# The expert stage made sparse: tokens sorted by expert on the chip, scattered, multiplied in tiles of one expert, gathered back

## The reference

```python
logits = x @ gate_w.T
scores = jax.nn.sigmoid(logits) + gate_bias
group_scores = scores.reshape(T, G, E // G).max(axis=-1)       # 8 groups of 8 experts
_, sel_groups = lax.top_k(group_scores, TG)                    # the best 4 groups
masked_scores = scores * mask                                  # the other groups at 0
topk_w, topk_i = lax.top_k(masked_scores, K)                   # K = 6
topk_w = topk_w / (topk_w.sum(axis=-1, keepdims=True) + 1e-08)
comb = jnp.zeros((T, E), x.dtype).at[jnp.arange(T)[:, None], topk_i].add(topk_w)
h = jax.nn.silu(jnp.einsum('th,eih->eti', x, eg_w)) * jnp.einsum('th,eih->eti', x, eu_w)
routed = jnp.einsum('eti,ehi,te->th', h, ed_w, comb)
return (shared + routed).reshape(B, S, H)
```

## Time and profile before

| | |
|---|---|
| median of 3 runs | 2080.95 us (2079.45 to 2091.61) |
| profiled execution, first to last instruction | 2082.6 us |
| PE, DVE, ACT, POOL busy | 93%, 71%, 64%, 47% of the span |
| expert stage, from the last update of the cross attention | 1493 to 2082.6 us |

### The profile page before, as it was taken

The page is one execution under the profiler, slowest core; times in us unless marked ns, Lnnn a source line. Parts: engine busy times, 40 slices in busy tenths (PEclk is TensorE's granted clock), DMA queues, the critical chain, the costliest instruction groups (busy, mean ns, idle before and its releaser), DMA issues.

```text
span 2082.6 us, 46757 instructions
## 1 busy us (share of the span) xinstructions
PE 1926.8 (93%) x15317; PEld 1548.1 (74%) x15317; DVE 1486.0 (71%) x3968; ACT 1336.5 (64%) x3090; POOL 971.7 (47%) x1173
## 2 busy tenths in 40 slices
PE   6999999999999999985089999999899999999998
PEld 4877778888888888852087878787677777777776
DVE  4668767777666666658977787666787788677775
ACT  4676567777776777657746767777555555555554
POOL 2555544444444444310017656444366566566565
PEclk8999999999999999998599999899899999999999
DMA  6533300000000000000033444555233333333333
GB/s 178 170 111 112 105 2 2 2 2 2 2 2 2 2 2 2 2 1 1 0 92 108 125 123 120 150 149 152 73 119 119 122 119 123 119 121 122 122 125 95
DMA packets 139169, 161.12 MB, mean 77 GB/s; under 512 B 15340, under 2 KB 99244, under 8 KB 138796
## 3 DMA queue, kind: packets, MB, share of 16 engines
q1 hardware_dynamic: 132780, 153.46, 24.5%
q10 hardware_dynamic: 6160, 4.78, 0.7%
HBM read 119.75 MB, written 38.70 MB: 76 GB/s over the span
## 4 chain that ended last, share of the span: by engine, by line
PE 68%; issue 8%; POOL 8%; DVE 6%; ACT 4%; SPq 3%; DMA 2%; ACTq 0%; POOLq 0%; DVEq 0%
POOL h_lo L2273 7%; PE bank L1010 6%; PE bank L1026 6%; PE score_banks L279 6%; PE score_banks L999 5%; PE bank L951 5%; PE bank L952 4%; PE bank L953 4%; PE bank L290 3%; PE score_banks L1930 3%; PE score_banks L1928 3%; PE score_banks L1929 3%; PE score_banks L261 3%; PE bank L1928 2%; PE bank L1929 2%
## 5 line engine op out<-in xcount | busy, mean ns | idle before, releaser
L2273 POOL TENSOR_TENSOR h_lo<-h,h_hi 128x512 fp32r<-128x512 f32 x264 | 341.5, 1294 | 243.3 <-ACT h_hi L2054 243.1
L1449 POOL TENSOR_TENSOR pw<-ew,rw 128x410 f32<-128x410 f32 x256 | 222.9, 871 | 368.7 <-DVE rw L1299 368.7
L2047 ACT ACTIVATE sl<-score_banks 128x512 f32<-128x512 f32 x264 | 157.9, 598 | 237.2 <-PE score_banks L1930 235.8
L459 ACT ACTIVATE pt<-score_banks 128x512 f32<-128x512 f32 (+1 forms) x384 | 230.0, 601 | 114.8 <-PE score_banks L279 113.8
L2192 DVE TENSOR_TENSOR bank<-score_banks,sl 128x512 f32<-128x512 f32 x264 | 184.1, 697 | 143.3 <-PE score_banks L1930 115.0
L1163 ACT ACTIVATE ew<-score_banks,nmax 128x205 f32<-128x205 f32 x512 | 217.8, 435 | 103.1 <-DVE nmax L1292 101.9
L573 DVE TENSOR_REDUCE nmx<-score_banks 128x4 fp32r<-128x512 f32 (+1 forms) x288 | 171.4, 596 | 121.4 <-PE score_banks L261 118.5
L725 POOL TENSOR_SCALAR_AFFINE_SELECT pt<-pt 128x512 f32<-128x512 f32 x256 | 165.2, 646 | 163.2 <-ACT pt L459 163.2
L279 PE MATMUL score_banks<-q_pack,k_diag 128*128 128x128 f32 (+1 forms) x1536 | 238.6, 279 | 0.4
L279 PEld LDWEIGHTS score_banks<-q_pack,k_diag 128*128 128x128 f32 (+1 forms) x1536 | 189.9, 181 | 46.4 <-issue 38.0
L1928 PE MATMUL score_banks<-x_hi,w_hi 128*128 128x512 f32 x528 | 209.9, 398 | 0.0
(11 more groups left out here) (353 smaller groups left out, 4694.6 us busy)
## 6 DMA issues: line engine op xcount, KB each, us to landing
share_b<-share_rows SPq DMA_DIRECT2D x256, 256.0 KB, 3.1
q_rows<-q_hi SPq DMA_DIRECT2D x96, 128.0 KB, 2.7
q_pack<-q_rows SPq DMA_DIRECT2D x32, 384.0 KB
raw<-in_experts SPq DMA_DIRECT2D x33, 192.0 KB, 3.1
q_rows<-q_lo SPq DMA_DIRECT2D x48, 128.0 KB, 2.8
k_diag<-k_rows SPq DMA_DIRECT2D x64, 96.0 KB
q_pack<-q_rows SPq DMA_DIRECT2D x31, 192.0 KB
k_diag<-k_rows SPq DMA_DIRECT2D x124, 48.0 KB
```

What stands on the lines that cost most here:

```text
L459: nc.scalar.activation(m.pt[0:a.keys, c, :, :].rearrange("p h t -> p (h t)"), m.flip[c % 2][0:a.keys, :], ACT.Exp).then_inc(s.exped.semaph ...
L1449: nc.gpsimd.tensor_tensor(m.pw[:, n, :, :], m.ew[:, n % 2, :, :], m.rw[:, n % 2, :].unsqueeze(2).broadcast_to([128, 2, KW]), ALU.mult)\
L2273: nc.gpsimd.tensor_tensor(m.h_lo[:, k % 3, :], m.h[:, (k + u) % 2, :], m.h_hi[:, k % 3, :].bitcast(F32), ALU.subtract).then_inc(s.los, 1)
```

## The change

Only the chosen experts are computed. The steps are these.

- The order of a group's choices is worked out by PE and DVE: matmuls with a triangle of ones and a square of ones (`ranks`) count, for each token and expert, how many tokens of the chunk stand before it; DVE adds each expert's start, rounded up to 128 rows, and takes the six slots per token with its max instruction (`starts`, `slots`). A table says which expert each tile of 128 rows belongs to (`list_tiles`, `table`).
- POOL scatters each normalised row to its six slots in DRAM: one indirect DMA of 128 rows for each sequence and choice, 192 in all (`scatter`). It later gathers the results the same way, 192 more (`gather`), into a ring of four sequences (`GBUFS`).
- The eight groups form four chunks (`SPANS`) of 1, 3, 3 and 1 groups. Since the number of tiles depends on the data, each chunk has room for the worst case: 11, 17, 17 and 11 rounds of eight tiles, 56 rounds in all, each always run.
- A round reads 8 tiles (512 KB), transposes them on PE, loads eight expert offsets into registers, projects with those as addresses, takes silu (ACT) and product (DVE), transposes the hidden values (four transposes for eight tiles), projects down and writes 512 KB back. All in plain float32, one expert per matmul of 128 columns: eight up, eight down.
- DVE finds each choice's share (`shares`) and adds the six gathered rows by their shares (`combine`), sequence b in round 34 + b up to sequence 21, the last ten after the rounds, beside the shared part, which now stands at the end.
- The slots are cleared once, by four DMAs from a tile of zeros that SP issues after attention 0 (`clear_slots`, 56 x 512 KB in all). The weights are loaded whole in 26 pieces; POOL splits nothing.

The core of the diff (the sorting's arithmetic is left out):

```diff
 def moe_tensor(pe, nc, m, s):
+    def tiles_in(n):
+        pe.wait_ge(s.tile_in[n % XBUFS], 16 * (n // XBUFS) + 16)
+        for k in range(2):
+            for i in range(4):
+                last = nc.tensor.transpose(m.turn[k][:, 128 * i:128 * i + 128], m.xr[:, n % XBUFS, 4 * k + i, :], m.ident[:])
+            last.then_inc(s.tiles_t, 1)
+    def gate_up(n):
...
+        _, experts[n] = nc.values_load_multi_w_load_instructions(
+            m.erow[0:1, chunk, TILES * r:TILES * r + TILES], engines=(mybir.EngineType.PE,), min_val=0, max_val=(E - 1) * F,
...
+        wait(pe, s.products, n)
+        for j in range(TILES):
...
+            last = nc.tensor.matmul(m.both[:, j // 4, j % 4, :, :], m.xt8[:, 128 * j:128 * j + 128],
+                                    m.gate_up[:, :, bass.ds(experts[n][j], F)], start=True, stop=True)
+    def body(n):
+        chunk, r = ROUNDS[n]
+        if r == 0:
+            tiles_in(n)
+        gate_up(n)
+        between(n)
+        if n < LAST_OF[chunk]:
+            tiles_in(n + 1)
+        if r > 0:
+            down(n - 1)
+        turn_hidden(n)
+        after(n)
+        if n == LAST_OF[chunk]:
+            down(n)
...
+        for n in range(NR):
+            if n == FIRST_OF[1]:
+                table(2)
+                ranks(7)
+                table(3)
+            body(n)
+        shared_tokens(0)
...
+            shared_gate_up(g)
+            if g + 1 < G:
+                shared_tokens(g + 1)
+            if g > 0:
+                shared_down(g - 1)
 def moe_vector(dve, nc, m, s, cross, link):
+    def combine(b, added=0):
+        wait(dve, s.shared_added, added)
+        dve.wait_ge(s.fetched[b % GBUFS], 16 * EK * (b // GBUFS) + 16 * EK)
+        for k in range(EK):
+            wait(dve, s.combined, EK * b + k)
+            nc.vector.scalar_tensor_tensor(tok(m.x, b), m.yk[:, b % GBUFS, k, :], m.wk[:, EK * b + k:EK * b + k + 1], tok(m.x, b),
+                                           ALU.mult, ALU.add).then_inc(s.combined, 1)
+    def after(n):
+        if n == 0:
+            for i in range(NORM_STEPS):
+                norm_alone(nc, m, link, m.stats, m.rstd, m.shift, 128, LATE, i)
+        elif n == 1:
+            for g in range(4, 8):
+                normalise(g)
+        if n in (AHEAD + 2, AHEAD + 4, AHEAD + 6):
+            rank(3 + (n - AHEAD) // 2)
+        if AHEAD <= n < AHEAD + 8:
+            first = ROUTE_STEPS // 2 * ((n - AHEAD) % 2)
+            for i in range(first, first + ROUTE_STEPS // 2):
+                route(4 + (n - AHEAD) // 2, i)
+        if 0 <= n - FIRST_OF[1] < 16:
+            shares(n - FIRST_OF[1])
+        if 0 <= n - FIRST_OF[2] < 16:
+            shares(16 + n - FIRST_OF[2])
+        if 0 <= n - FIRST_OF[2] - 6:
+            combine(n - FIRST_OF[2] - 6)
     def run():
+        normalise(1)
+        rank(0)
+        starts(0)
+        list_tiles(0)
+        slots(0)
...
+        normalise(2)
+        normalise(3)
+        keep_table(0)
+        for n in range(ROUTE_STEPS):
+            route(1, n)
+        for g in (2, 3):
+            for n in range(ROUTE_STEPS):
+                if n == 4:
+                    rank(g - 1)
+                route(g, n)
+        rank(3)
+        starts(1)
+        list_tiles(1)
+        for g in (1, 2, 3):
+            slots(g)
+        keep_table(1)
+        for n in range(NR):
+            if n == FIRST_OF[1]:
+                rank_last()
+            body(n)
...
 def moe_pool(pool, nc, m, s):
+    def scatter(g):
+        pool.wait_ge(s.slotted, g + 1)
+        for q in range(GB):
+            for k in range(EK):
+                at = (GB * g + q) * EK + k
+                nc.gpsimd.indirect_dma_start(
+                    out=m.slots_in[chunk_of(g)], out_offset=bass.IndirectOffsetOnAxis(ap=m.idx[:, at:at + 1], axis=0),
+                    in_=m.xh[:, GB * g + q, :], in_offset=None).then_inc(s.sent[chunk_of(g)], 16)
+    def gather(b):
+        chunk = chunk_of(b // GB)
+        if b == GB * SPANS[chunk][0]:
+            for v in range(YBUFS):
+                pool.wait_ge(s.tile_out[v], 16 * len(range(v, LAST_OF[chunk] + 1, YBUFS)))
+        wait(pool, s.combined, EK * (b - GBUFS) + EK)
...
+    def run():
+        pool.wait_ge(s.blanked, 16 * len(SPANS))
+        for g in range(G):
+            scatter(g)
+        for b in range(B):
+            gather(b)
 def moe_sync(sp, m, s, out, x_view):
+    for chunk in range(len(SPANS)):
+        load(FIRST_OF[chunk])
+        load(FIRST_OF[chunk] + 1)
+        for n in range(FIRST_OF[chunk], LAST_OF[chunk] + 1):
+            if n + 2 <= LAST_OF[chunk]:
+                load(n + 2)
+            if n > FIRST_OF[chunk]:
+                store(n - 1)
+        store(LAST_OF[chunk])
```

More of the change, by code:

```diff
@@ new lines, in ranks @@
+    def ranks(g):
+        misc_read()
+        pe.wait_ge(m.s.route, ROUTE_STEPS * g + ROUTE_STEPS - 1)
+        if g == 0:
+            pe.wait_ge(s.tables_in, m.tables_loads)
+        chosen = lambda q: m.selb[:, g % 2, q * E:q * E + E]
+        for q in range(GB):
+            nc.tensor.matmul(m.misc[:, q * E:q * E + E], m.before[:], chosen(q), start=True, stop=q == 0)
+            for earlier in range(q):
+                nc.tensor.matmul(m.misc[:, q * E:q * E + E], m.every[:], chosen(earlier), start=False, stop=earlier == q - 1)
+        for q in range(GB):
+            last = nc.tensor.matmul(m.misc[:, GB * E:GB * E + E], m.every[:], chosen(q), start=q == 0, stop=q == GB - 1)
+        last.then_inc(s.ranked, 1)
+        due["placed"] = g + 1
@@ new lines, in turn_hidden, with down @@
+    def turn_hidden(n):
+        pe.wait_ge(s.products, n + 1)
+        for p in range(TILES // 2):
+            last = nc.tensor.transpose(m.bank[2][:, 128 * p:128 * p + 128], m.h[:, 0, 128 * p:128 * p + 128], m.ident[:])
+        last.then_inc(s.hidden_t, 1)
+    def down(n):
+        pe.wait_ge(s.hidden_s, 2 * n + 2)
+        wait(pe, s.low_tiles, n)
+        wait(pe, s.high_tiles, n)
+        for j in range(TILES):
+            out = m.out_bank[j // 4][:, 128 * (j % 4):128 * (j % 4) + 128].rearrange("p (a c) -> p a c", a=2)
+            last = nc.tensor.matmul(out, m.ht[:, j % 2, 128 * (j // 2):128 * (j // 2) + 128],
+                                    m.down[:, :, bass.ds(experts[n][j], F)], start=True, stop=True)
+            if j % 4 == 3:
+                last.then_inc(s.downed, 1)
@@ new lines, in silu, with hidden, low_tiles @@
+    def silu(n):
+        act.wait_ge(s.projected, n + 1)
+        nc.scalar.activation(m.sl[:].rearrange("p (j f) -> p j f", f=F), m.gates, ACT.Silu).then_inc(s.silus, 1)
+    def hidden(n):
+        act.wait_ge(s.hidden_t, n + 1)
+        for k in range(2):
+            half = slice(F * k, F * k + F)
+            nc.scalar.copy(m.ht[half, k, :], m.bank[2][half, :]).then_inc(s.hidden_s, 1)
+    def low_tiles(n):
+        act.wait_ge(s.downed, 2 * n + 1)
+        wait(act, s.tile_out[n % YBUFS], 16 * (n // YBUFS))
+        nc.scalar.copy(m.yr[:, n % YBUFS, 0:4, :].rearrange("p j c -> p (j c)"), m.out_bank[0][:]).then_inc(s.low_tiles, 1)
@@ new lines, in list_tiles, with keep_table @@
+    def list_tiles(chunk):
+        wait(dve, s.tabled, chunk)
+        for k in range(2):
+            last = nc.vector.tensor_scalar(m.passed[:, k, :], m.ends[:], m.iota[:, k:k + 1], None, ALU.is_le)
+        link(last)
+        link(nc.vector.tensor_reduce(m.etab[:], m.passed[:], AX.X, ALU.add))
+        nc.vector.tensor_scalar(m.etab[:], m.etab[:], float(E - 1), float(F), ALU.min, ALU.mult).then_inc(s.listed, 1)
+    def keep_table(chunk):
+        dve.wait_ge(s.tabled, chunk + 1)
+        nc.vector.tensor_copy(m.erow[0:1, chunk, :], m.misc[0:1, 0:256]).then_inc(s.tables, 1)
@@ L2252, in tail @@
                 route(0, n)
+        if b == 31:
+            wait(dve, cross.measured, 24)
+            for n in range(3 * c, min(3 * c + 3, NORM_STEPS)):
+                norm_alone(nc, m, link, m.stats, m.rstd, m.shift, 128, MIDDLE, n)
     def run():
-        over_groups(dve, body)
-        hidden(G - 1, 1, NT - 1)
-        update(G - 1)
+        normalise(1)
[3 more added lines that the diff above has]
+        slots(0)
+        for k in range(2):
+            nc.vector.memset(m.ht[F * (1 - k):F * (1 - k) + F, k, :], 0.0)
@@ new lines, in run, with rank_last @@
+        done = NR - FIRST_OF[2] - 6
+        for g in range(G):
+            shared_product(g)
+            if g > 0:
+                shared_add(g - 1, done + g)
+            combine(done + g, g)
+        shared_add(G - 1, done + G)
+        for b in range(done + G, B):
+            combine(b, G)
+    def rank_last():
+        starts(2)
+        list_tiles(2)
+        for g in (4, 5, 6):
+            slots(g)
+        keep_table(2)
+        rank(7)
+        starts(3)
+        list_tiles(3)
+        slots(7)
+        keep_table(3)
@@ L2770, in program @@
         alibi_rows = nc.dram_tensor("alibi_slopes", (128 - DATA, H * T), F32, kind="Internal").ap()
```

(3 more changed lines are left out.)

707 lines of the change are left out of this document (375 added, 332 removed).

## The result

The changed kernel takes 2002.24 us in the median (1999.07 to 2003.06), the kernel before 2083.11 beside it: a ratio of 0.960, 95% interval 0.958 to 0.963, so 4.0% or 81 us less. I had forecast 2043. On some other chips the same kernel takes 2325 to 2333 us; the last part of the experiments is about that, and up to there every profile, and every conclusion, is from chips where it takes 2000 to 2020.

What follows compares the result with a forecast made beforehand. PE was taken to bound the expert stage; 1493 + 64 lead-in + 83 chunk 0 + 24 stop + 297 rounds + 24 chunk changes + 4 drain + 54 tail = 2043 us; likeliest case 2010 to 2060, 8-in-10 range 1985 to 2180.

Steps and rivals of the forecast that it cites:

- the round at 6.6 us: Expert stage: one round takes PE 5.2 us of matmuls and transposes plus 1.4 us for waits and register loads; 45 rounds, 297 us.
- Lead-in: Between cross attention and first product: DVE normalises, routes groups 1 to 3, ranks and works out slots, 64 us, nothing hiding it.
- Chunk 0: First chunk's rounds run slower because DVE still has routings, ranks and normalisings beside them: 83 us, to 1640.
- Stop at round 11: After chunk 0, `rank_last` stops DVE and PE waits for its tables: 20 us plus 4 until the next product, at 1664.
- Chunk changes: The other two changes of chunk: SP's load stands behind the last store, leaving 12 us open each.
- P: POOL's time to issue one indirect DMA, taken as 1.15 us; DVE would not wait for gathers until about 1.3.
- Rival (a): POOL's queue becomes the bound, ending at 1646 + 288 P + 10; 2100 to 2290 us, chance 0.20.
- rival (c): Everything is cheap: P = 0.6 and a round 5.7 us, ending at 1983; under 2010 us, chance 0.12.
- Tail: After the rounds, ten sequences still to be added, with remaining gathers, landing, additions and store: 54 us, PE's shared part hidden.
- Contention of POOL and DVE: In the expert stage, DVE might slow POOL's descriptor writing as wide operations were slowed, bringing P near 1.9.
- Rival (b): Registers and address computations on PE cost time, a round up to 9.3 us; 2100 to 2190 us, chance 0.15.
- Rival (d): Uncounted waits, chunk changes of 20 us or routings at 13 us, bring it within 1% of before; 2060 to 2100, chance 0.15.

## Why the prediction was right and wrong

The sign was right, the size half: 38 us forecast, 81 measured. The step that failed is the round at 6.6 us, and with it the choice of the path that sets the end: PE's rounds in the forecast, POOL's queue in the runs. By its own steps:

- **Lead-in, 64 us, first product at 1557.** DVE's first product stands at 1539.6, 49.9 us behind the cross attention (which ended 3.3 us sooner, at 1489.7). The routings were taken too long. One measured 8.0 us against my 11.3, three of them 10 of the 14 us; three times `slots` at 2.5 us in place of 3.6 are 3 more:

```profile
1502.52 0.42 DVE L2249 TENSOR_TENSOR ms<-sc,gq 128x256 f32<-128x256 f32 x1
...
1503.97 0.42 DVE L2259 TENSOR_TENSOR se<-ms,m 128x256 f32<-128x256 f32 x1
```

  Wide operations take 0.42 us here, with POOL issuing DMAs beside them. In the routing of the earlier trace rows four of them took 0.92, 1.22, 1.50 and 1.10 us, while POOL split weights; here the same four take 0.43, 0.42, 0.68 and 0.42. DVE and POOL in the kernel before:

```profile
1477.08 1.22 DVE L2169 TENSOR_TENSOR se<-ms,m 128x256 f32<-128x256 f32 x1
...
1476.96 1.05 POOL L865 TENSOR_TENSOR w_lo<-raw,w_hi 128x384 fp32r<-128x384 f32 x1
```

  I carried a slowdown from rows whose neighbour the change removes.
- **Chunk 0, 83 us:** 82.4 (1539.6 to 1622.0). **Stop at round 11, 24 us:** 1622.0 to the next product at 1642.4, 20.5. **Chunk changes, 12 us:** 10.9. All near.
- **The round, 6.6 us. This is the term that failed:** 4.88 measured in chunk 1, so 45 x 1.7 = 77 us too much. Of it 1.4 us were for waits and register loads, which cost nothing in steady rounds (the run without the register work has the same period), and 0.3 for the matmuls and transposes: 16 x 0.224 + 12 x 0.108 = 4.88 (a `gate_up` of 8 matmuls, two records each, takes 1.79; 0.108 is what is left for a transpose). I let DVE wait for gathers only from about P = 1.3, since I set 6 P against a round of 6.6; against 4.88 it waits at the measured P already, 49.3 us in all.
- **P, 1.15 us for an indirect DMA:** 1.25 to 1.27, of which 0.94 to 0.96 is the instruction and 0.30 the issue behind it. The bound "issue of the same kind" was near; that the gap comes on top I did not see.
- **Rival (a), POOL becomes the bound,** is what happened, with my formula: 1646 + 288 P + 10 with the start at 1627 in place of 1646. I weighed it at 0.20 and only as the slower side, because I compared P with a round of 6.6 us. The sum with the lead-in (17), the stop (3.5) and the rounds (77) put right would be 2043 - 98 = 1945; POOL's queue ends at 2000.6, 56 us later. No run shows the 1945 itself: in each POOL still set the end. Against it POOL is the bound from P = 1.07 on (1627 + 288 P + 9 against 1945), below even my own 1.15. So the error in the round did two things: it hid 77 us of gain, and it hid what takes most of it back. That 2002 lies inside the range is in part luck, since the two offset each other. By its number it falls to rival (c), under 2010, but (c) had P = 0.6 and was half right only: the rounds were cheap, the DMAs were not.
- **Tail, 54 us:** 80 us from the last product (1920.8 for the last `down`). It is no longer a tail of 10 sequences but what POOL had still to issue.
- **Contention of POOL and DVE,** P near 1.9: not seen. A scatter is 0.958 us in the median of 192 (the longest took 1.8), with DVE busy 68% (1540 to 1640) or 57% (1640 to 1725) beside it, and a gather 0.944 beside DVE's additions. The Trainium skill (GPSIMD Engine Reference, Specifications) lets GpSimd contend with vector instructions of two SBUF inputs. The kernel before agrees, where DVE's operation of 1.22 us above ran beside POOL's arithmetic; for indirect DMAs on POOL the trace after does not, with 0.42 us beside them.
- **Rival (b), registers:** fell. One of my arguments against it did not hold, though: in the loop over groups of the kernel before, PE's queue computes counts for its semaphores (128 operations of 32 ns), but none stands at the matmuls' lines 1928 to 1930; no address of an operand is computed there. **Rival (d), waits not counted:** the chunk changes and the routings came out shorter, not longer. **Clearing the slots hidden:** right as far as the trace goes (DMA is at 9 and 7 tenths in slices 6 and 7 alone, long before the scatters); no run took it away.
- The Trainium skill's price (DMA: Bandwidth & Descriptors, Latency and other measured facts), about 1 us for the first byte of a DMA issued by GpSimd: the 0.94 to 0.96 us that POOL spends on one are near it, though a latency is not a price per DMA, and the step from one to the next is 1.26.

## What to carry to other kernels

When a change puts hundreds of small DMAs on one queue, sum that queue as an engine of its own (count x step from issue to issue, from the moment its first input is there) before anything else, and compare it with the other engines' sums at their lower bounds too: a pessimistic cost for one engine hides the next one. Register loads and addresses on PE's queue cost nothing here while matmuls were queued ahead of them (4.88 us a round with and without). And run a kernel that leans on GpSimd's DMAs on several chips before believing its time.

## What the runs showed of the hardware

- An indirect DMA of 128 rows of 512 bytes takes POOL 0.944 us (gather) or 0.958 us (scatter) and 0.30 us until the next; with 64 rows 0.899 us. A gather lands 2.7 us after its issue in the median.
- The same program with the same data took 2002 to 2010 us in three sets and 2325 to 2333 in two, on other chips, where ScalarE's instructions stand 11.2 or 22.4 us apart during streams of indirect DMAs; a kernel without them took 2080 to 2085 on all.
- Eight float32 matmuls of 128 columns take 1.79 us at clock 1.00, and a round of chunk 1 takes 4.88 us, with or without addresses from registers.
